# A two-layer decoder on one core: attention scores in four 64x64 tiles, normalisation after the value product, stage loops written out

## The chip, the cores and the metric

The kernel runs on one core of a Trainium2 chip. The metric is device time in microseconds for one execution. The kernel before takes 2339.52 us (median of three runs, 2339.38 to 2343.82). Engines are named as in the profile: PE is TensorE, PEld its weight loads, DVE VectorE, ACT ScalarE, POOL GpSimd, SP SyncE, and ACTq the queue from which ScalarE issues transfers.

## The reference

Sixty-four sequences of 64 tokens with 128 channels go through six sublayers, each with a residual: self-attention (16 heads of 8 channels, rotary, causal), a gated linear attention, a mixture of 15 routed experts and a shared one, self-attention with distance biases, a cross-attention, and a soft mixture of experts. The change is in the two self-attentions:

```python
scores = jnp.einsum('bhqd,bhkd->bhqk', q, k) / jnp.sqrt(jnp.float32(HEAD_DIM))
scores = scores + causal
attn = jax.nn.softmax(scores, axis=-1)
out = jnp.einsum('bhqk,bhkd->bhqd', attn, v)
out = out.transpose(0, 2, 1, 3).reshape(B, S, D_MODEL)
return out @ wo + bo
```

Layer 0 has biases on q, k, v and the output; layer 1 has none, but a term that falls with distance inside `scores`.

## The kernel before, in words

The 4096 tokens are 32 tiles of 128 rows, two sequences (b = 0, 1) in each. The stages follow one another: load and normalise (`load_and_norm`, lines 104 to 226), `attention` of layer 0, `mlstm`, `experts`, `attention` of layer 1, `cross_attention`, `soft_experts`. Each is a block in which every engine has its own program, written by hand as `turn(t, u)`, and engines meet only by semaphores. A turn works on several tiles at once, one step of each: it is a software pipeline whose order is the order of the code.

The first five of these stages are walked by one of two helpers. `unrolled` writes every turn out. `turns` writes out the first `head * ring` turns and the last `tail * ring`, and puts those between into a hardware loop (`Fori`) whose body is `ring` turns; there, tile numbers and semaphore counts come from registers. `load_and_norm` (ring 8), both attentions (ring 4, head 2, tail 2: turns 8 to 23 are looped), `mlstm` (ring 4, turns 8 to 27) and `experts` (8 groups of four tiles, ring 2, groups 2 to 5) use `turns`. `cross_attention` uses `unrolled`.

In turn t of `attention` the steps that matter here are:

- PE: transposes of the probabilities of tile t-1 (line 378, into `p_t[0]` and `p_t[1]`); output projection of tile t-2 (389); q and k of tile t+4 (400); v of tile t+2 (409); probabilities times values of tile t-1 (424, into `p_o`); a transpose for the normalised result (295); scores of tile t+2 (440 and 442). The scores have one buffer only: banks `p_s[0]` (heads 0 to 7) and `p_s[1]` (heads 8 to 15). Line 440 adds mask and bias and may not start before ACT has read the tile before out of the bank (semaphore `exped`). Line 442 multiplies q (64 rows of a sequence, 128 channels) by `kblk`, which holds k once for each of the 16 heads with all other heads' channels at zero, so that a contraction over 128 channels gives one head's score.
- DVE: row maxima of tile t+1 (459, 461) and the centring of the second half (465); residual of tile t-2 (472 adds the output bias in layer 0, 474 adds the projection); statistics; row sums of the second half of tile t (482); rotary terms of tile t+4 in layer 0 (491); 1/sum (498, 16 numbers a row); normalisation (285); probabilities of tile t times 1/sum (505, 1024 columns).
- ACT: copies of `p_t[0]` and `p_t[1]` of tile t-1 to `pT` (553, two of 512 columns); eight exponentials of tile t+1 with running sums (562); one exponential over the second half (566); in layer 1 the copies of q and k (573, 574); v to its blocks (582); `p_o` to `oT` of tile t-1 (590 or 592); input copy (598); `xnT` (301, 303).
- POOL: `kblk` of tile t+3, two instructions of 1024 columns (531), and 1/sqrt for the normalisation (271, 274).

Of the kernel before, what the change touches and what calls it, by code (L numbers as in the profile page):

```python
# [22 lines left out]
P = 128  # L23
B, S, D = 64, 64, 128
# [9 lines left out]


def turns(eng, turn, first, last, ring, n=NT, head=1, tail=1):

    for t in range(first, head * ring):
        turn(t, t % ring)
    with eng.Fori(head, n // ring - tail) as i:  # L40
        for u in range(ring):
            turn(i * ring + u, u)
    for t in range(n - tail * ring, last):
        turn(t, t % ring)
# [69 lines left out]
def load_and_norm(nc, g, io):  # L114
# [3 lines left out]
    with Mem(nc, "ld") as m:  # L118
# [20 lines left out]
        def _(dve):  # L139
# [26 lines left out]
            turns(dve, turn, -1, NT, R)  # L166

        @block.gpsimd
        def _(pool):
# [10 lines left out]
            turns(pool, turn, 0, NT, R)  # L180

        @block.tensor
        def _(pe):
# [12 lines left out]
            turns(pe, turn, 0, NT, R)  # L196

        @block.scalar
        def _(act):
# [26 lines left out]
            turns(act, turn, 0, NT, R)  # L226
# [86 lines left out]
def attention(nc, g, io, layer):  # L313
# [3 lines left out]
    with Mem(nc, f"at{layer}") as m:  # L317
        w = {n: m.sb(n, [P, P]) for n in names}
        heads = m.sb("heads", [P, NH])
# [5 lines left out]
        if rope:  # L325
# [22 lines left out]
        summed, inverted, probs_ready = m.sem("summed"), m.sem("inverted"), m.sem("probs_ready")  # L348
        pt_done, pt_copied, pv_done, oT_copied, y_done = (m.sem(n) for n in ("pt_done", "pt_copied", "pv_done", "oT_copied", "y_done"))
# [14 lines left out]
        def _(pe):  # L364
            pe.wait_ge(consts_in, 16 * len(loads))
            pe.wait_ge(zeroed, 1)
            wv = w["wv"][:, :].rearrange("i (j h d) -> i h j d", j=NH // 2, h=2)

            def turn(t, u):
                k, v = t - 1, (u - 1) % R  # L370
                if has(k):

                    pe.wait_ge(probs_ready, k + 1)
                    for hf in range(2):
                        if has(k - 1):
                            pe.wait_ge(pt_copied, 2 * k + hf - 1)
# [3 lines left out]
                        mm.then_inc(pt_done, 1)  # L380
                k = t - 2
                if has(k):

                    pe.wait_ge(oT_copied, k + 1)
# [18 lines left out]
                if has(k):  # L403

                    if has(k - 1):
                        pe.wait_ge(v_copied, 2 * k)
                    for h in range(2):
# [5 lines left out]
                if has(k):  # L413

                    pe.wait_ge(v_copied, 2 * (k + 1))
                    if has(k - 1):
                        pe.wait_ge(oT_copied, k)
                    pe.wait_ge(pt_copied, 2 * k + 2)
                    for c in range(4):
                        for b in range(PER):  # L420
# [12 lines left out]
                if has(k):  # L433
# [3 lines left out]
                    for hf in range(2):  # L437
# [8 lines left out]
            turns(pe, turn, first, last, R, head=2, tail=2)  # L446

        @block.vector
        def _(dve):
            dve.memset(vblk[:, :, :, :, :], 0.0).then_inc(zeroed, 1)  # L450
            dve.wait_ge(consts_in, 16 * len(loads))

            def turn(t, u):
                k, v = t + 1, (u + 1) % R
                if has(k):

                    scores = [p_s[hf][:, :].rearrange("p (h k) -> p h k", h=HH) for hf in range(2)]
# [1585 lines left out]
```

## Time and profile before

| | before |
|---|---|
| median of three runs | 2339.52 us |
| profiled execution, device time | 2340.49 us |
| its span | 2338.5 us |
| PE busy | 2044.0 us (87%) |
| DVE busy | 1645.1 us (70%) |
| ACT busy | 1514.4 us (65%) |
| POOL busy | 1249.6 us (53%) |

The span is the time from the first to the last instruction of the profile; device time has 2.0 us more around it. The busy time of PE is modelled: each matmul's end is an estimate, so ends overlap the next start, and the difference between two starts is what one step costs. An idle time in square brackets is shown before the instruction that ended it, with the instruction that it waited for.

### The profile page before, as it was taken

The numbers are of one execution on the slowest core, as the hardware profiler recorded it, in microseconds if no ns is written. First come the engines' busy times: TensorE is split into PE (matmuls) and PEld (weight loads), VectorE is DVE, ScalarE is ACT, GpSimd is POOL, SyncE is SP. The second block draws the span as 40 slices with busy tenths as digits, with TensorE's granted clock in tenths as the row PEclk, the third lists the DMA queues.
The fourth block names the chain that finished last, engine by engine and source line by source line (L and its number), as shares of the span: only waits on it lengthen the run. The fifth ranks groups of instructions, "written<-read, shape, count | busy, mean of one in ns | idle before, by whom it ended". The sixth has DMA issues, their size and how long they took to land. (4 is left out here: it accounts for less than half of the span.)

```text
span 2338.5 us, 64508 instructions
## 1 busy us (share of the span) xinstructions
PE 2044.0 (87%) x23034; PEld 1539.3 (66%) x23034; DVE 1645.1 (70%) x4478; ACT 1514.4 (65%) x4433; POOL 1249.6 (53%) x1444
## 2 busy tenths in 40 slices
PE   4899976646999999978996999996699999999899
PEld 2566563324666666745554888885588888888777
DVE  7799829976666666547775666665777777777567
ACT  4577726637777778857774777774776666666642
POOL 5777504445777778867773233320854544445430
PEclk9999956558999999989998999998899999999999
DMA  3000020011000000000000000001000000000101
GB/s 87 4 1 0 1 41 1 0 37 50 1 1 1 0 0 1 1 11 2 0 1 29 2 2 2 2 2 61 5 5 14 16 5 14 16 3 14 50 3 39
DMA packets 48919, 30.71 MB, mean 13 GB/s; under 512 B 21886, under 2 KB 46350, under 8 KB 48398
## 3 DMA queue, kind: packets, MB, share of 16 engines
q1 hardware_dynamic: 39438, 22.98, 3.5%
q10 hardware_dynamic: 9216, 4.20, 0.7%
q8 instruction: 166, 2.72, 0.5%
q14 instruction: 99, 0.81, 0.1%
HBM read 22.97 MB, written 4.19 MB: 12 GB/s over the span
## 5 line engine op out<-in xcount | busy, mean ns | idle before, releaser
L1006 POOL TENSOR_TENSOR ff_hl<-ff_hid,ff_hh 128x512 fp32r<-128x512 f32 x272 | 353.4, 1307 | 114.3 <-ACT ff_hh L1245 108.1
L1855 POOL TENSOR_TENSOR sm_zsum<-sm_zsum,sm_logits 128x512 f32<-128x512 f32 x120 | 154.7, 1289 | 275.3 <-ACT sm_logits L1881 273.6
L531 POOL TENSOR_TENSOR at_kblk<-at_kT,at_heads 128x1024 f32<-128x1024 f32 x128 | 242.0, 1912 | 101.5 <-PE at_p_s L442 91.8
L1174 DVE TENSOR_TENSOR ff_hid<-ff_p_b,ff_hid 128x512 f32<-128x512 f32 x240 | 164.3, 685 | 157.5 <-ACT ff_hid L1234 156.9
L1234 ACT ACTIVATE ff_hid<-ff_p_h,ff_b 128x512 f32<-128x512 f32 x272 | 185.6, 682 | 48.5 <-PE ff_p_h L1062 45.4
L1898 ACT ACTIVATE sm_sT<-sm_p_s 128x512 f32<-128x512 f32 x128 | 69.5, 595 | 221.1 <-PE sm_p_s L1691 221.1
L1245 ACT ACTIVATE ff_hh<-ff_hid 128x512 fp32r<-128x512 f32 x272 | 170.2, 626 | 40.8 <-DVE ff_hid L1174 38.7
L1867 POOL TENSOR_TENSOR sm_logits<-sm_logits,sm_peak 128x512 f32<-128x512 f32 x128 | 162.9, 1294 | 12.4 <-ACT sm_comb L1916 11.7
L1705 PE MATMUL sm_p_l<-g_phi,g_xnT 128*128 128x256 f32 x512 | 142.3, 405 | 26.8 <-ACT sm_logits L1926 25.6
L562 ACT ACTIVATE at_pr<-at_p_s,at_small 128x64 f32<-128x64 f32 x512 | 152.7, 341 | 4.6 <-DVE at_small L459 4.6
L1060 PE MATMUL ff_p_h<-ff_xh,ff_w1h 128*128 128x512 f32 x272 | 134.9, 496 | 12.1 <-ACT ff_hid L1234 8.5
L553 ACT ACTIVATE at_pT<-at_p_t 128x512 f32<-128x512 f32 x128 | 69.6, 595 | 112.8 <-PE at_p_t L378 112.8
L442 PE MATMUL at_p_s<-at_kblk,at_qT 128*64 128x512 f32 x512 | 139.5, 623 | 0.0
L1739 PE MATMUL sm_p_y<-sm_w,sm_sT 128*32 128x128 f32 x4096 | 125.4, 274 | 9.1 <-ACT sm_combT L1888 8.4
L1804 DVE TENSOR_REDUCE sm_rmax<-sm_p_l 128x2 f32<-128x512 f32 x128 | 88.3, 690 | 62.4 <-PE sm_p_l L1705 61.7
L1747 PE MATMUL sm_p_o<-sm_yy,sm_combT 128*64 128x129 f32 x2048 | 127.9, 276 | 2.5 <-issue 1.9
L1705 PEld LDWEIGHTS sm_p_l<-g_phi,g_xnT 128*128 128x128 f32 x512 | 91.1, 197 | 55.2 <-ACT sm_logits L1926 28.4
L1739 PE MATMUL sm_p_s<-sm_w,sm_sT 128*32 128x128 f32 x4096 | 124.1, 273 | 0.2 <-issue 0.2
L1739 PEld LDWEIGHTS sm_p_y<-sm_w,sm_sT 128*32 128x32 f32 x4096 | 107.6, 110 | 22.7 <-ACT sm_sT L1898 11.6
L1836 DVE TENSOR_TENSOR sm_yy<-sm_p_y,sm_wb 128x512 f32<-128x512 f32 x128 | 88.1, 692 | 49.1 <-PE sm_p_y L1739 49.0
L1747 PEld LDWEIGHTS sm_p_o<-sm_yy,sm_combT 128*64 128x64 f32 x2048 | 110.4, 136 | 17.1 <-DVE sm_yy L1836 13.3
L562 ACT ACTIVATION_READ_ACCUMULATOR at_pr<-at_p_s,at_small 128x1 f32 x512 | 120.6, 235 | 0.0
(302 smaller groups left out, 6079.8 us busy)
## 6 DMA issues: line engine op xcount, KB each, us to landing
sm_w<-in_w_soft SPq DMA_DIRECT2D x8, 512.0 KB, 3.6
ff_whole<-in_L_ffn_rW SPq DMA_DIRECT2D x30, 128.0 KB, 2.7
early_xs<-in_x ACTq DMA_DIRECT2D x32, 64.0 KB, 1.9
ld_ctx<-in_ctx ACTq DMA_DIRECT2D x32, 64.0 KB, 2.1
ml_vals<-in_ctx SPq DMA_DIRECT2D x8, 256.0 KB, 4.9
x_kept<-early_xs SPq DMA_DIRECT2D x1, 2048.0 KB, 7.4
g_xnT<-x_kept SPq DMA_DIRECT2D x1, 2048.0 KB, 9.4
out_x<-sm_acc SPq DMA_DIRECT2D x8, 256.0 KB, 2.3
```

Of the source, the lines that this page charges most:

```text
L442: mm = pe.matmul(p_s[hf][S * b:S * b + S, :], qT[:, v, b * S:(b + 1) * S], kblk[:, v % 2, b, hf * half:(hf + 1) * half], start=False, stop ...
L531: op = pool.tensor_tensor(kblk[:, v % 2, b, :].rearrange("p (h k) -> p h k", h=NH), row_bc(kT[:, v, b * S:(b + 1) * S], NH), col_bc(heads[ ...
L562: op = act.activation(pr[:, v, h * S:(h + 1) * S], p_s[0][:, h * S:(h + 1) * S], ACT.Exp, bias=small[:, v, 0, h:h + 1], accum_out=small[:, ...
L1006: eng.tensor_tensor(hl[:, q, :], hid[:, q, :], hh[:, q, :].bitcast(F32), ALU.subtract).then_inc(h_split, 1)
L1174: dve.tensor_tensor(h, p_b[e % 2][:, :], h, ALU.mult).then_inc(scaled, 1)
L1234: act.activation(hid[:, slot(u, c), :], p_h[c % 2][:, :], ACT.Gelu, bias=b1[:, c:c + 1]).then_inc(gelud, 1)
L1245: act.activation(hh[:, q, :], hid[:, q, :], ACT.Copy).then_inc(h_rounded, 1)
L1705: mm = pe.matmul(p_l[h][:, a * CW:(a + 1) * CW], xnT[:, t * P:(t + 1) * P], phi[:, c % 2, :], start=True, stop=True)
L1739: mm = pe.matmul((p_y, p_s)[j % 2][a][SP * k:SP * (k + 1), (b * CQ + q) * D:(b * CQ + q + 1) * D], sT[:, j % 2, a, b, n_ * SP:(n_ + 1) * S ...
L1747: mm = pe.matmul(p_o[j % 2][b * S:(b + 1) * S, a * E1:a * E1 + D + 1], combT[:, j % RING_C, q, a, b * S:(b + 1) * S], yy[:, j % 2, a * PER ...
L1855: pool.tensor_tensor(z, z, logits[:, j % RING_L, :, :], ALU.add).then_inc(summed, 1)
L1867: pool.tensor_tensor(here, here, row_bc(peak[:, c % 2, :], TU), ALU.subtract).then_inc(centred, 1)
```

## The change

It has three parts.

1. Scores. `kblk` is half as wide: heads 0 to 7 lie on partitions 0 to 63, heads 8 to 15 on partitions 64 to 127, 512 columns per sequence instead of 1024. PE adds mask and bias to both banks, then issues four matmuls of 64 rows by 64 columns of the array: row half hf writes bank `p_s[hf]`, column half b writes the rows of sequence b. `s_done` counts once per tile instead of twice. The constant `c_heads` has 8 columns.
2. Normalisation. The multiplication of the probabilities (line 505 of before) is gone. The reciprocal is written eight times for each head (`inv`, 128 columns instead of 16), PE transposes it by a matmul with the identity into `p_o[:, P:2P]`, ACT copies that to `invT`, and DVE multiplies the value product by it (`oT`), in place of ACT's copy of `p_o`. ACT takes the second `pT` copy between the fourth and the fifth exponential. In layer 0 the value bias goes into the output bias once, ahead of the loop, and POOL adds that bias to the residual.
3. Loops. `turns` is deleted; all five stages that used it are written out with `unrolled`. Semaphore counts and addresses become constants.

```diff
-            turns(dve, turn, -1, NT, R)
+            unrolled(dve, turn, -1, NT, R)
...
+        inv, invT = m.sb("inv", [P, 2, NH, HD]), m.sb("invT", [P, P])
...
-                    pe.wait_ge(probs_ready, k + 1)
                     for hf in range(2):
+                        pe.wait_ge(c_exped if hf else exped, k + 1)
...
+                    pe.wait_ge(inverted, k + 1)
+                    if has(k - 1):
+                        pe.wait_ge(oT_made, k)
+                    pe.matmul(p_o[:, P:2 * P], inv[:, v % 2, :, :].rearrange("p h d -> p (h d)"), g["ident"][:, :],
+                              start=True, stop=True).then_inc(inv_turned, 1)
...
-                        for b in range(PER):
-                            mm = pe.matmul(p_s[hf][S * b:S * b + S, :], qT[:, v, b * S:(b + 1) * S],
-                                           kblk[:, v % 2, b, hf * half:(hf + 1) * half], start=False, stop=True)
-                        mm.then_inc(s_done, 1)
+                    for b in range(PER):
+                        for hf in range(2):
+                            rows = slice(S * hf, S * hf + S)
+                            mm = pe.matmul(p_s[hf][S * b:S * b + S, :], qT[rows, v, b * S:(b + 1) * S],
+                                           kblk[rows, v % 2, b, :, :].rearrange("p h k -> p (h k)"), start=False, stop=True)
+                    mm.then_inc(s_done, 1)
...
-                    dve.reciprocal(small[:, v, 2, :], small[:, v, 1, :]).then_inc(inverted, 1)
+                    if has(k - 2):
+                        dve.wait_ge(inv_turned, k - 1)
+                    dve.reciprocal(inv[:, v % 2, :, :], col_bc(small[:, v, 1, :], HD)).then_inc(inverted, 1)
+                k = t - 1
+                if has(k):
+                    dve.wait_ge(pv_done, k + 1)
...
+                    dve.tensor_tensor(oT[:, (u - 1) % 2, :], p_o[:, 0:P], invT[:, :], ALU.mult).then_inc(oT_made, 1)
...
-                    dve.tensor_tensor(pr[:, v, :].rearrange("p (h k) -> p h k", h=NH), pr[:, v, :].rearrange("p (h k) -> p h k", h=NH),
-                                      col_bc(small[:, v, 2, :], S), ALU.mult).then_inc(probs_ready, 1)
...
+                turn_copy(t - 1, (u - 1) % 2, 0)
+                if has(t - 1):
+                    act.wait_ge(inv_turned, t)
...
+                    act.activation(invT[:, :], p_o[:, P:2 * P], ACT.Copy).then_inc(inv_copied, 1)
                 k, v = t + 1, (u + 1) % R
...
+                exps(k, v, range(HH // 2), False)
+                turn_copy(t - 1, (u - 1) % 2, 1)
+                exps(k, v, range(HH // 2, HH), True)
```

How this moves instructions in a steady turn of layer 0, engine by engine. On PE, from the scores of one tile to the projection, before (`at_` is the attention's prefix, `at0_` that of its semaphores in layer 0):

```order
L440 MATMUL at_p_s<-at_bias,at_pick 128x512 [waits at0_exped,at0_kblk_ready,at0_q_ready]
L442 MATMUL at_p_s<-at_kblk,at_qT 64x512 x2
L440 MATMUL at_p_s<-at_bias,at_pick 128x512 [waits at0_centred]
L442 MATMUL at_p_s<-at_kblk,at_qT 64x512 x2
L378 MATMUL at_p_t<-g_ident,at_pr 128x128 [waits at0_pt_copied,at0_probs_ready]
L378 MATMUL at_p_t<-g_ident,at_pr 128x128 x3
L378 MATMUL at_p_t<-g_ident,at_pr 128x128 [waits at0_pt_copied]
L378 MATMUL at_p_t<-g_ident,at_pr 128x128 x3
L389 MATMUL at_p_y<-at_wo,at_oT 128x128 [waits at0_n_copied,at0_x_made,at0_oT_copied]
```

and the same place of the changed kernel:

```order
L444 MATMUL at_p_s<-at_bias,at_pick 128x512 [waits at0_exped,at0_kblk_ready,at0_q_ready]
L444 MATMUL at_p_s<-at_bias,at_pick 128x512 [waits at0_centred]
L448 MATMUL at_p_s<-at_kblk,at_qT 64x512 x4
L374 MATMUL at_p_t<-g_ident,at_pr 128x128 [waits at0_pt_copied,at0_exped]
L374 MATMUL at_p_t<-g_ident,at_pr 128x128 x3
L374 MATMUL at_p_t<-g_ident,at_pr 128x128 [waits at0_pt_copied,at0_c_exped]
L374 MATMUL at_p_t<-g_ident,at_pr 128x128 x3
L381 MATMUL at_p_o<-g_ident,at_inv 128x128 [waits at0_oT_made,at0_inverted]
L391 MATMUL at_p_y<-at_wo,at_oT 128x128 [waits at0_n_copied,at0_x_made,at0_oT_made]
```

The four score matmuls stand together behind both bias matmuls, the transposes wait for ACT instead of DVE, and the transposition of 1/sum has come in ahead of the projection. On ACT, from the copies of `p_t` to the exponential of the second half, before:

```order
L553 ACTIVATE at_pT<-at_p_t 128x512 [waits at0_pv_done,at0_pt_done]
L550 REGISTER_ALU
L553 ACTIVATE at_pT<-at_p_t 128x512 [waits at0_pv_done,at0_pt_done]
L558 ISA
L562 ACTIVATE at_pr,at_small<-at_p_s,at_small 128x64 [waits at0_pt_done,at0_maxed]
L562 ACTIVATE at_pr,at_small<-at_p_s,at_small 128x64 x7
L566 ACTIVATE at_pr<-at_pr 128x512 [waits at0_centred]
```

and after:

```order
L569 ACTIVATE at_pT<-at_p_t 128x512 [waits at0_pv_done,at0_pt_done]
L588 ACTIVATE at_invT<-at_p_o 128x128 [waits at0_oT_made,at0_inv_turned]
L578 ACTIVATE at_pr,at_small<-at_p_s,at_small 128x64 [waits at0_pt_done,at0_maxed]
L578 ACTIVATE at_pr,at_small<-at_p_s,at_small 128x64 x3
L569 ACTIVATE at_pT<-at_p_t 128x512 [waits at0_pv_done,at0_pt_done]
L578 ACTIVATE at_pr,at_small<-at_p_s,at_small 128x64 [waits at0_pt_done,at0_maxed]
L578 ACTIVATE at_pr,at_small<-at_p_s,at_small 128x64 x3
L595 ACTIVATE at_pr<-at_pr 128x512 [waits at0_centred]
```

A copy of 128 columns that waits for PE's new matmul stands ahead of the exponentials, and the second `pT` copy stands between them. On DVE, the end of a turn, before:

```order
L498 RECIPROCAL at_small<-at_small 128x16 [waits at0_summed]
L285 TENSOR_SCALAR at_n_xn<-early_xs,at_n_mv,at_n_rstd 128x128 [waits at0_n_rstd_made0,at0_n_transposed]
L505 TENSOR_TENSOR at_pr<-at_pr,at_small 128x1024 [waits at0_inverted]
L459 TENSOR_REDUCE at_small<-at_p_s 128x8 [waits at0_s_done]
L461 TENSOR_REDUCE at_small<-at_p_s 128x8 [waits at0_s_done]
```

and after:

```order
L508 RECIPROCAL at_inv<-at_small 128x128 [waits at0_inv_turned,at0_summed]
L514 TENSOR_TENSOR at_oT<-at_p_o,at_invT 128x128 [waits at0_y_done,at0_pv_done]
L274 TENSOR_SCALAR at_n_xn<-early_xs,at_n_mv,at_n_rstd 128x128 [waits at0_n_rstd_made0,at0_n_transposed]
L469 TENSOR_REDUCE at_small<-at_p_s 128x8 [waits at0_s_done]
L470 TENSOR_REDUCE at_small<-at_p_s 128x8
```

The pass over 1024 columns is gone, the reciprocal has eight times the columns, and DVE has a new wait for PE's value product.

## Rows read from the trace of the kernel before

**Rows 1.** Windows: length, PE, PEld, DVE, ACT, POOL busy, clock, DMA.

```profile
130.00:241.30 111.30, 109.33 (x1105) 68.79 (x1104) 106.26 (x273) 81.52 (x385) 85.62 (x97) 1.00 0.00 1
380.00:480.00 100.00, 69.08 (x327) 33.94 (x327) 94.45 (x595) 60.75 (x232) 50.37 (x96) 0.55 0.00 0
```

**Rows 2.** Timeline, PE, one turn of layer 0: start, length, matmul records.

```profile
150.76 0.38 PE L440 MATMUL at_p_s<-at_bias,at_pick 128*128 128x512 bf16 x1
151.07 1.08 PE L442 MATMUL at_p_s<-at_kblk,at_qT 128*64 128x512 f32 x4
152.08 0.39 PE L440 MATMUL at_p_s<-at_bias,at_pick 128*128 128x512 bf16 x1
...
153.41 1.09 PE L378 MATMUL at_p_t<-g_ident,at_pr 128*128 128x128 f32 x8
154.34 0.39 PE L389 MATMUL at_p_y<-at_wo,at_oT 128*128 128x128 f32 x2
...
157.69 0.38 PE L440 MATMUL at_p_s<-at_bias,at_pick 128*128 128x512 bf16 x1
```

**Rows 3.** Timeline, ACT, the same turn; the last from layer 1.

```profile
154.10 1.09 ACT L553 ACTIVATE at_pT<-at_p_t 128x512 f32<-128x512 f32 x2 [1.79 <-PE at_p_t L378]
155.07 0.32 ACT L562 ACTIVATE at_pr<-at_p_s,at_small 128x64 f32<-128x64 f32 x1
...
1154.34 0.28 ACT L592 ACTIVATE at_oT<-at_p_o 128x128 f32<-128x128 f32 x1
```

**Rows 4.** Timeline, PE, first and last tile's first bias matmul, each layer.

```profile
70.62 0.61 PE L440 MATMUL at_p_s<-at_bias,at_pick 128*128 128x512 bf16 x1
...
282.69 0.38 PE L440 MATMUL at_p_s<-at_bias,at_pick 128*128 128x512 bf16 x1 [0.74 <-ACT at_pr L562]
...
1028.67 0.59 PE L440 MATMUL at_p_s<-at_bias,at_pick 128*128 128x512 bf16 x1
...
1245.71 0.38 PE L440 MATMUL at_p_s<-at_bias,at_pick 128*128 128x512 bf16 x1 [0.73 <-ACT at_pr L562]
```

**Rows 5.** Timeline, PE, in the cross-attention.

```profile
1405.32 0.40 PE L1386 MATMUL xa_pj<-xa_wvh,xa_zh 128*128 128x512 f32 x1
1405.56 0.39 PE L1387 MATMUL xa_pj<-xa_wvl,xa_zh 128*128 128x512 f32 x1
...
1406.54 1.10 PE L1333 MATMUL xa_p_s<-xa_kT,xa_qT 64*64 64x128 f32 x32
1407.58 0.33 PE L1344 MATMUL xa_p_t<-g_ident,xa_pr 128*128 128x128 f32 x1
```

**Rows 6.** Groups by shape: count, busy, mean ns, idle before, what ended it.

```profile
L1788 DVE RECIPROCAL sm_rz<-sm_p_l 128x256 f32<-128x256 f32 x8 | 14.1, 1757 | 5.6 <-PE sm_p_l L1676 5.6
```

**Rows 7.** Timeline, DVE, layer 0.

```profile
151.72 1.49 DVE L505 TENSOR_TENSOR at_pr<-at_pr,at_small 128x1024 f32<-128x1024 f32 x1
```

**Rows 8.** Waits, PE for DVE, while layer 0's attention drains (283:304).

```profile
PE at_p_t L378 <- DVE at_pr L505: 3.5, 2, 1.8
```

**Rows 9.** Timeline, PE, load stage: two written-out turns, then one looped.

```profile
16.29 0.45 PE L192 MATMUL ld_tp<-g_ident,ld_xn 128*128 128x128 f32 x1
...
18.32 0.45 PE L192 MATMUL ld_tp<-g_ident,ld_xn 128*128 128x128 f32 x1
...
25.14 0.48 PE L192 MATMUL ld_tp<-g_ident,ld_xn 128*128 128x128 f32 x1 [0.60 <-ACT early_cnT L223]
...
26.64 0.48 PE L192 MATMUL ld_tp<-g_ident,ld_xn 128*128 128x128 f32 x1 [0.60 <-ACT early_cnT L223]
```

**Rows 10.** Waits, DVE, looped part of `mlstm`: us in total, times, longest.

```profile
DVE ml_dd L758 <- issue: 1.7, 4, 0.4
```

**Rows 11.** Timeline, PE, experts: first hidden matmul of groups 2, 6, 7.

```profile
659.32 0.49 PE L1060 MATMUL ff_p_h<-ff_xh,ff_w1h 128*128 128x512 f32 x1 [0.18 <-ACT ff_hid L1234]
...
892.91 0.50 PE L1060 MATMUL ff_p_h<-ff_xh,ff_w1h 128*128 128x512 f32 x1
...
950.88 0.50 PE L1060 MATMUL ff_p_h<-ff_xh,ff_w1h 128*128 128x512 f32 x1
```

More of the change, by code:

```diff
@@ L33, in has @@
     return not isinstance(k, int) or 0 <= k < n
[L36 to L44, printed above, removed]
 def unrolled(eng, turn, first, last, ring):
@@ L178, in turn @@
                 pool.tensor_tensor(rstd[:, u, :], rstd[:, u, :], g["neghalf"][:, 0:2], ALU.pow).then_inc(rstd_made, 1)
-            turns(pool, turn, 0, NT, R)
+            unrolled(pool, turn, 0, NT, R)
         @block.tensor
@@ L194, in turn @@
                 pe.transpose(bank[:, 2 * P:3 * P], cn[:, u, :], g["ident"][:, :]).then_inc(transposed, 1)
-            turns(pe, turn, 0, NT, R)
+            unrolled(pe, turn, 0, NT, R)
         @block.scalar
@@ L224, in turn @@
                                scale=g["gbx"][:, 0:1]).then_inc(copied, 1)
-            turns(act, turn, 0, NT, R)
+            unrolled(act, turn, 0, NT, R)
 class Norm:
@@ L366, in _ @@
             pe.wait_ge(zeroed, 1)
+            if rope:
+                pe.wait_ge(bv_spread, 1)
+                pe.matmul(p_v[:, 0:D], bvb[:, :], w["wo"][:, :], start=True, stop=True).then_inc(bv_done, 1)
             wv = w["wv"][:, :].rearrange("i (j h d) -> i h j d", j=NH // 2, h=2)
@@ L502, in turn @@
                     norm.dve_norm(dve, t - 3, (u - 1) % 2, 1)
-                if has(k):
-                    dve.wait_ge(inverted, k + 1)
-                    dve.tensor_tensor(pr[:, v, :].rearrange("p (h k) -> p h k", h=NH), pr[:, v, :].rearrange("p (h k) -> p h k", h=NH),
-                                      col_bc(small[:, v, 2, :], S), ALU.mult).then_inc(probs_ready, 1)
-            turns(dve, turn, first, last, R, head=2, tail=2)
+            unrolled(dve, turn, first, last, R)
         @block.gpsimd
@@ L537, in turn @@
                     norm.pool_rstd(pool, t - 3, (u - 1) % 2, 1)
-            turns(pool, turn, first, last, R, head=2, tail=2)
+            unrolled(pool, turn, first, last, R)
         @block.scalar
@@ L600, in turn @@
                     norm.act_copy(act, t - 2 - levels, p_y[:, P:2 * P])
-            turns(act, turn, first, last, R, head=2, tail=2)
+            unrolled(act, turn, first, last, R)
 MH, MD = 4, 32
@@ L719, in turn @@
                     mm.then_inc(pv_done, 1)
-            turns(pe, turn, first, last, R, head=2)
+            unrolled(pe, turn, first, last, R)
         @block.vector
@@ L827, in turn @@
                     norm.dve_stats(dve, n, w)
-            turns(dve, turn, first, last, R, head=2)
+            unrolled(dve, turn, first, last, R)
         @block.gpsimd
@@ L853, in turn @@
                     norm.pool_rstd(pool, t - 3, (u - 1) % 2)
-            turns(pool, turn, first, last, R, head=2)
+            unrolled(pool, turn, first, last, R)
         @block.scalar
@@ L905, in turn @@
                     norm.act_copy(act, t - 5, p_n[:, 0:P])
-            turns(act, turn, first, last, R, head=2)
+            unrolled(act, turn, first, last, R)
 NE, TOPK = 15, 3
@@ L1103, in turn @@
                         pe.transpose(p_n[:, 0:P], norm.xn[:, q % 2, 0, :], g["ident"][:, :]).then_inc(norm.transposed, 1)
-            turns(pe, turn, first, last, R, NGR)
+            unrolled(pe, turn, first, last, R)
         FIRST_SPLIT = {-1: [NC_FF - 1], 0: [1, 2, 3, 4]}
@@ L1186, in turn @@
                         router[c - 5]()
-            turns(dve, turn, first, last, R, NGR)
+            unrolled(dve, turn, first, last, R)
         @block.gpsimd
@@ L1197, in turn @@
                     split_hidden(pool, t, u, c)
-            turns(pool, turn, first, last, R, NGR)
+            unrolled(pool, turn, first, last, R)
         @block.scalar
@@ L1259, in turn @@
                         norm.act_copy(act, 4 * (t - 1) + AT_LNT.index(c), p_n[:, 0:P])
-            turns(act, turn, first, last, R, NGR)
+            unrolled(act, turn, first, last, R)
 XH, XD = 8, 64
```

85 lines of the change are left out of this document (47 added, 38 removed).

## The prediction, made before the changed kernel ran

> **What bounds the kernel now.** I read the windows by stage first, then one turn of an attention on each engine, then the prices of what is new. In the looped part of layer 0's attention PE is busy 109 of 111 us and DVE 106 of 111 [rows 1], so either could pass for the limit. The timeline shows a third thing, a circle through one buffer. Follow one turn. PE starts the first bias matmul at 150.76 and the transposes 2.65 us later, at 153.41 [rows 2]; four of them release ACT's first copy at 154.10, 0.69 later; the two copies take 0.97 up to the first exponential at 155.07 [rows 3]; and the last exponential frees the bank for PE's next bias matmul at 157.69, 2.62 later [rows 2, 3]. The sum, 2.65 + 0.69 + 0.97 + 2.62 = 6.93, is the whole turn. Nothing in it is idle, and PE's other work (projection, q, k, v, value product) lies beside it. Where there is less of that work the wait is in the open: PE idles 0.74 and 0.73 us for ACT's exponentials before the last tile's scores of each layer [rows 4]. From first to last tile, 31 intervals, layer 0 takes 212.07 us and layer 1 217.04 [rows 4]. The 4.97 us more in layer 1 I put down to transposes that wait for DVE's 1024-column pass, as they openly do at the end of layer 0 (3.5 us in two waits [rows 8]).
>
> **The score part.** Now a bias matmul, two tiles of 64 columns side by side, and both once more: 2.65 us. After: bias, bias, four tiles. Two 512-column matmuls of one mode that follow each other start 0.24 apart (1405.32, 1405.56 [rows 5]); from a bias matmul to tiles it is 0.31, and two tiles take 1.01 (151.07 to 152.08) [rows 2]. Whether four take the same is the open price. Two matmuls of 512 columns in 1.01 us are 0.126 us per matmul of 128 columns, two at a time. The cross-attention issues 16 matmuls of 64x64 with 128 columns (32 records, two a matmul), to two banks in the same pattern: at two at a time they would take 2.02 us, and they take 1.04 (1406.54 to 1407.58 [rows 5]). So four run side by side, and I take 1.01; the other bound is 2.02. Scores: 0.24 + 0.31 + 1.01 = 1.56, that is 1.09 less.
>
> The Trainium skill (TensorEngine Tiling, Key Properties) says that changing the tiling mode drains the array; the trace agrees in that 0.31 stands where the mode changes and 0.24 where it doesn't. Without that rule the second bias matmul would be 0.31 and the turn 0.07 longer, some 4 us in all.
>
> **What comes into the circle.** PE's transposition of 1/sum stands where the projection stood, 0.93 us behind the start of the transposes (153.41 to 154.34), and is 0.39 long like it [rows 2]. The release of ACT costs 0.06: eight transposes in 1.09 end 0.28 behind their last start, so the fourth ends at 0.63, and ACT starts at 0.69 [rows 2, 3]. The copy of 1/sum can thus start at 1.56 + 0.93 + 0.39 + 0.06 = 2.94. The first `pT` copy starts at 1.56 + 0.69 = 2.25 and takes half of 0.97, up to 2.73; ACT idles 0.21. The new copy of 128 columns is 0.28 long [rows 3]; copies start 0.11 sooner than they are long (0.60 against 0.485 [rows 3]), so 0.17: 3.11. The exponentials take 2.62 and the second `pT` copy between them 0.49: 6.22. That is the turn I forecast, 0.71 less than 6.93. The value product needs the second copy, which now is done 0.6 us later than the first half of the product would like it; its first half covers that.
>
> **Do the others fit into 6.22?** PE: 6.93 less 1.09, plus some 0.25 for the new matmul, is 6.1. DVE is busy 106.26 / 16 = 6.64 a turn [rows 1]. It loses 1.49 (the 1024-column pass [rows 7]) and the bias add, at least an eighth of that, 0.19. It gains a multiplication of 128 columns, some 0.3, and seven eighths of a reciprocal of 128 columns. A reciprocal is dear: 1757 ns for 256 columns [rows 6], half is 0.88, so 0.8 more. Sum 6.1, close below. POOL is busy 85.62 / 16 = 5.35 [rows 1] and halves its largest instruction. ACT, 81.52 / 16 = 5.1 [rows 1], swaps one copy for another.
>
> **Attentions, summed.** The first three intervals of a layer are a ramp without all parts of the circle; I leave them as they are. Layer 0: 28 x 0.71 = 19.9 us. Layer 1: the same and the 4.97 us, since transposes no longer wait for DVE: 24.9. At the drain of each layer 3.5 us of waits for the pass [rows 8] go, and a reciprocal longer by 0.7 takes their place: 2.8 each, 5.6. The folded bias costs a DVE copy and a matmul ahead of layer 0's first q, which nothing hides: 0.6 against me. Together 49.8.
>
> **Loops written out.** In the load stage ACT issues two transfers a turn between its copies. Written-out turns there take (18.32 - 16.29) / 2 = 1.015 us; looped ones, with the same work and with addresses from registers, 1.50 (25.14 to 26.64), and PE waits for ACT [rows 9]. All 16 looped turns become written-out ones: 7.8 us. This is no detail of the attentions and the surest term. In `mlstm` DVE is the limit (94 of 100 us [rows 1]) and loses 1.7 us at four loop ends [rows 10]. In the experts four looped groups take (892.91 - 659.32) / 4 = 58.40 and a written-out one 950.88 - 892.91 = 57.97 [rows 11]: 1.7. Together 11.2. That written-out code costs anything itself I see nowhere: the load stage and the experts run both kinds, and the written-out one is never slower [rows 9, 11].
>
> **The sum.** 49.8 + 11.2 = 61.0 us. The profiled execution took 2340.5 us (span 2338.5 and 2.0 around it), so 2279.5; it lay 1.0 above the median of the three runs, so the forecast is 2278.5.
>
> **Rivals.**
>
> 1. *Another engine closes in.* DVE's 6.1 is within 0.1 of the circle, built on lengths of one trace; its new wait for the value product stands ahead of the normalisation. At 6.4 to 6.8 a turn the gain shrinks by 60 x 0.2 to 0.6: 2290 to 2313. For it: the narrow margin. Against: the pass that leaves DVE was its longest. Chance 0.20.
> 2. *Less than 6.22.* If ACT doesn't idle the 0.21 and layer 1, with two q and k matmuls fewer, runs more freely, 6.0: another 13 us, 2265. Chance 0.15.
> 3. *Tiles of 512 columns share something that tiles of 128 don't.* Then 2.02 instead of 1.01: a turn is 7.23, 0.30 above now; layer 0 loses 8.4, layer 1 (7.11 now) 3.4, and with drains, loops and the folded bias 2340.5 + 11.8 - 5.6 - 11.2 + 0.6 = 2336, less 1.0: 2335. Nothing in the trace speaks for it but that it isn't shown. Chance 0.03.
> 4. *Reading the banks decides, not writing them.* If the circle went only through ACT, quicker scores would bring nothing and 0.38 would be added: 7.31 a turn, 28 x 0.38 + 28 x 0.20 = 16.2 lost there, 2339.5. PE's first bias matmul starts right behind the last exponential in every turn, which speaks against it. The Trainium skill (TensorEngine Tiling, PSUM Bottleneck) warns of this: tiles speed up the array but not the emptying of its banks. Chance 0.02.
> 5. *The clock, on the slow side.* With PE 69 of 100 us busy in `mlstm` its granted clock is 0.55, about the lower level of 1.2 GHz; in the attention it is 1.00 [rows 1]. If four tiles for one count as less work and the clock falls, PE's 6.1 a turn become about 11, +4 a turn against now, from a fifth of the 60 turns on slower than before; in half of them 2340 + 120 - 17 = about 2440. Against: the cross-attention has such tiles, and PE stays some 95% busy. Chance 0.03.
>
> The forecast keeps 0.57.
>
> **How the numbers follow.** A measurement of this kernel tells from no change what is over 0.2%, 4.7 us. Faster: forecast, 1 and 2 with 0.92 and half of 3, 0.94 in all; within 0.2%: the rest of 3 and 4, 0.03; slower 0.03. Range: a turn of 6.0 in both layers gives 2265, of 6.5 gives 2295; drains and folded bias add some 3 either way. With part of rival 1 I give 2262 to 2304.
>
> **What would show each step.** The first bias matmuls of neighbouring tiles 6.2 us apart in both layers; 32-tile spans of about 192 us; four score tiles in 1.0 us; a reciprocal of 0.8 to 1.0 us; ACT's `invT` copy behind a wait of 0.2 for PE; turns of 1.0 us throughout the load stage, which then ends near 44 instead of 52 us; no issue gap on DVE in `mlstm`. The prediction is wrong if score tiles take 2 us, if PE's first bias matmul is released by something else than the last exponential, if DVE has no idle time in a turn, or if the clock in an attention falls.

## The result, and the profile after

The changed kernel takes 2278.3 us (median of four runs, 2276.1 to 2279.0), against 2339.5 us before. The ratio is 0.9731, with a 95% interval of 0.9718 to 0.9743: 61 us faster by the medians, 63 by the ratio (60 to 66). The forecast was 2278.5. The total fits better than its terms: two errors of about 5 us nearly cancel, and that is luck. Stages end where ACT starts its last copy into `g_xnT` (the last one with the span):

| stage | before | after | difference | forecast |
|---|---|---|---|---|
| load | 51.4 | 48.0 | -3.3 | -7.8 |
| attention 0 | 253.8 | 227.5 | -26.2 | -22.1 |
| mlstm | 209.7 | 209.4 | -0.3 | -1.7 |
| experts | 501.6 | 500.0 | -1.6 | -1.7 |
| attention 1 | 255.1 | 226.5 | -28.5 | -27.7 |
| cross-attention | 334.4 | 334.3 | -0.1 | 0 |
| soft experts | 732.6 | 730.8 | -1.8 | 0 |

The last two stages were not touched. In the ten other kernels below the last one lies between 728.3 and 732.8 us, so its 1.8 here says nothing, and one profile doesn't settle differences of a few us in so long a stage.

**The circle.** PE's rows of one turn of layer 0, to be laid beside [rows 2] (start, length, matmul records), with the row of the weight loads ahead:

```profile
147.83 0.13 PEld L444 LDWEIGHTS at_p_s<-at_bias,at_pick 128*128 128x128 bf16 x2 [0.29 <-issue]
...
148.08 0.38 PE L444 MATMUL at_p_s<-at_bias,at_pick 128*128 128x512 bf16 x1 [0.35 <-POOL at_qT L532]
148.38 1.09 PE L448 MATMUL at_p_s<-at_kblk,at_qT 64*64 64x512 f32 x8
149.40 1.09 PE L374 MATMUL at_p_t<-g_ident,at_pr 128*128 128x128 f32 x8
150.33 0.39 PE L381 MATMUL at_p_o<-g_ident,at_inv 128*128 128x128 f32 x2
...
154.25 0.38 PE L444 MATMUL at_p_s<-at_bias,at_pick 128*128 128x512 bf16 x1 [0.34 <-POOL at_qT L532]
```

There are two weight loads of L444 but one matmul: the record of the first bias matmul is missing, and the row at 148.08 is the second. I therefore date the first by its weight load, 147.83. (In the kernel before, where both records are there, the weight load at 150.73 starts 0.03 ahead of its matmul.) Four tiles take 1.02 us (148.38 to 149.40; forecast 1.01), the scores 1.54 to 1.57 in all (forecast 1.56), and from turn to turn it is 6.17 (148.08 to 154.25; forecast 6.22). ACT in the same turn, beside [rows 3]:

```profile
147.46 0.26 ACT L578 ACTIVATION_READ_ACCUMULATOR at_pr<-at_p_s,at_small 128x1 f32 x1
...
150.09 0.60 ACT L569 ACTIVATE at_pT<-at_p_t 128x512 f32<-128x512 f32 x1 [0.80 <-PE at_p_t L374]
150.75 0.28 ACT L588 ACTIVATE at_invT<-at_p_o 128x128 f32<-128x128 f32 x1
150.93 0.31 ACT L578 ACTIVATE at_pr<-at_p_s,at_small 128x64 f32<-128x64 f32 x1
...
152.09 0.62 ACT L569 ACTIVATE at_pT<-at_p_t 128x512 f32<-128x512 f32 x1
```

The first copy starts 0.69 behind the transposes, the copy of 1/sum 0.66 later (its idle time, 0.18, is what is left of 0.66 when the first copy's 0.485 is taken off), the exponentials 0.18 after that. The last exponential ends at 147.72, and PE's next weight load starts at 147.83. The profile puts PE's idle time down to POOL's `qT`, which is a misreading: POOL is two tiles ahead of PE there, so the q for these scores was made two turns earlier, and in layer 1 the same gap is put down to ACT's exponentials (below, 1191.08). First and last tile of each layer, beside [rows 4]:

```profile
67.85 0.63 PE L444 MATMUL at_p_s<-at_bias,at_pick 128*128 128x512 bf16 x1 [0.33 <-issue]
...
259.20 0.38 PE L444 MATMUL at_p_s<-at_bias,at_pick 128*128 128x512 bf16 x1 [0.35 <-ACT at_pr L578]
...
997.60 0.63 PE L444 MATMUL at_p_s<-at_bias,at_pick 128*128 128x512 bf16 x1 [0.33 <-issue]
...
1191.08 0.38 PE L444 MATMUL at_p_s<-at_bias,at_pick 128*128 128x512 bf16 x1 [0.35 <-ACT at_pr L578]
```

31 intervals take 191.4 and 193.5 us, 20.7 and 23.6 less than before; the layers now differ by 2 us only, from their first three turns.

**The other engines.** Windows of after, layer 0 and layer 1 (columns as in [rows 1]), and DVE's rows that answer to the prediction's prices:

```profile
120.00:250.00 130.00, 122.73 (x1479) 91.89 (x1498) 115.93 (x337) 109.99 (x507) 86.56 (x148) 1.00 0.01 2
1030.00:1180.00 150.00, 137.21 (x1593) 97.34 (x1618) 126.61 (x412) 138.92 (x630) 83.91 (x145) 1.00 0.01 2
```

```profile
147.81 0.94 DVE L508 RECIPROCAL at_inv<-at_small 128x128 f32<-128x128 f32 x1
148.67 0.23 DVE L514 TENSOR_TENSOR at_oT<-at_p_o,at_invT 128x128 f32<-128x128 f32 x1
...
149.54 0.69 DVE L469 TENSOR_REDUCE at_small<-at_p_s 128x8 f32<-128x512 f32 x1 [0.39 <-PE at_p_s L448]
```

The reciprocal takes 0.94 us (0.86 from row to row, forecast 0.88). DVE has 0.39 idle in each turn of layer 0 (8.1 us in 21 turns) and about 0.48 in layer 1, waiting for the scores, and the clock stays at 1.00.

### The profile page after: what moved, and what is told of

Same layout as the page of the kernel before. It is cut to its first block and busy times, and to the rows that moved or that the text cites. A ratio compares the mean times of both kernels' runs of the same rounds, so it can differ in the third digit from the quotient of the medians.

```text
span 2276.6 us, 62556 instructions
## 1 busy us (share of the span) xinstructions
PE 1997.3 (88%) x23071; PEld 1551.1 (68%) x23164; DVE 1593.3 (70%) x4448; ACT 1525.7 (67%) x4433; POOL 1152.6 (51%) x1476
## 5 line engine op out<-in xcount | busy, mean ns | idle before, releaser
L543 POOL TENSOR_TENSOR at_kblk<-at_kT,at_heads 128x512 f32<-128x512 f32 x128 | 130.7, 1042 | 106.5 <-PE at_p_s L448 96.9
L1759 PEld LDWEIGHTS sm_p_s<-sm_w,sm_sT 128*32 128x32 f32 x4096 | 113.4, 110 | 2.3 <-issue 2.3
L428 PE MATMUL at_p_o<-at_pT,at_vblk 128*32 128x64 f32 x2048 | 104.5, 222 | 9.8 <-ACT at_pT L569 8.6
```

The lines of the kernel that those rows point to most:

```text
L543: op = pool.tensor_tensor(kblk[:, v % 2, b, :, :], row_bc(kT[:, v, b * S:(b + 1) * S], HH), col_bc(heads[:, :], S), ALU.mult)
L1759: mm = pe.matmul((p_y, p_s)[j % 2][a][SP * k:SP * (k + 1), (b * CQ + q) * D:(b * CQ + q + 1) * D], sT[:, j % 2, a, b, n_ * SP:(n_ + 1) * S ...
```

## The experiments

Each ratio is to the kernel before on the same chip; "us" behind a ratio is its difference from 1 (or from another ratio) times 2339.5. A difference of two ratios carries both intervals, 4 to 5 us either way for most pairs here; where it is smaller than that, only the stages and turns in the profiles speak. Turns are read from PE's rows.

**Loops alone** (e1), the kernel before with `unrolled` in all stages:

```diff
-            turns(dve, turn, first, last, R, head=2, tail=2)
+            unrolled(dve, turn, first, last, R)
```

> The kernel before with every loop written out, nothing else. From the trace of after, the stages that only lost their loops gave 3.4 us (load), 0.3 (mlstm) and 1.7 (experts); the attentions' turns that end a loop are 0.08 longer than the others, some 1 us in all. So 6 us less than before, about 2333.5 (2331 to 2335). The prediction's terms would make it 11.2 less, 2328. If it is 2339, writing out brings nothing and the stages differ for another reason.

Ratio 0.9969 (0.9957 to 0.9981): 7.3 us, 4.4 to 10.1. The forecast's 11.2 lies outside. By itself the interval doesn't say whether it is 5 or 10; the load stage ends at 48.3, as in the changed kernel, and `mlstm` takes 209.3 us, as there (209.4).

**Scores alone** (e2), on top of e1: four tiles, the 1024-column pass kept.

```diff
-                        for b in range(PER):
-                            mm = pe.matmul(p_s[hf][S * b:S * b + S, :], qT[:, v, b * S:(b + 1) * S],
-                                           kblk[:, v % 2, b, hf * half:(hf + 1) * half], start=False, stop=True)
+                    for b in range(PER):
+                        for hf in range(2):
+                            rows = slice(S * hf, S * hf + S)
+                            mm = pe.matmul(p_s[hf][S * b:S * b + S, :], qT[rows, v, b * S:(b + 1) * S],
+                                           kblk[rows, v % 2, b, :, :].rearrange("p h k -> p (h k)"), start=False, stop=True)
```

> The kernel before with loops written out and the score tiles of after; the probabilities are still scaled by the 1024-column pass. My theory: two limits lie close together, the circle (6.93 less 1.09 = 5.84) and DVE's own work with the pass in it. DVE then sets the turn: about 6.65 in layer 0 and 6.45 in layer 1 (5.55 busy and 0.9 of waits for POOL), in all 28 us less than with loops written out alone: 2305 (2298 to 2318). If the parts of the change simply add up, the scores bring 56 x 1.09 = 61 us: 2272. If PE's score time were worth nothing, 2333.

Ratio 0.9807 (0.9789 to 0.9826): 38 us less than e1, more than the 28 that I expected and far from 61. Layer 0 takes 6.62 a turn (expected 6.65), with DVE never waiting: 123.71 of 130 us busy, the rest being the distances between its instructions. One row shows more than my sum had:

```profile
130.00:260.00 130.00, 108.69 (x1316) 78.28 (x1333) 123.71 (x333) 99.05 (x466) 97.06 (x119) 1.00 0.01 2
```

```profile
181.58 0.67 DVE L473 TENSOR_TENSOR early_xs<-early_xs,at_bo 128x128 f32<-128x128 f32 x1
182.28 0.29 DVE L475 TENSOR_TENSOR early_xs<-at_p_y,early_xs 128x128 f32<-128x128 f32 x1
```

Two additions of one size, 0.67 and 0.29 long; the long one has both operands in SBUF and lies beside POOL's `kblk` (180.06 to 182.10). Layer 1 takes 6.18, not 6.45: there DVE isn't the limit, but a circle of 5.84 in which the transposes wait a little for the pass:

```profile
1099.98 0.38 PE L440 MATMUL at_p_s<-at_bias,at_pick 128*128 128x512 bf16 x1 [0.78 <-ACT at_pr L563]
1100.29 1.09 PE L444 MATMUL at_p_s<-at_kblk,at_qT 64*64 64x512 f32 x8
1101.65 1.09 PE L378 MATMUL at_p_t<-g_ident,at_pr 128*128 128x128 f32 x8 [0.27 <-DVE at_pr L506]
...
1106.16 0.38 PE L440 MATMUL at_p_s<-at_bias,at_pick 128*128 128x512 bf16 x1 [0.78 <-ACT at_pr L563]
```

I had counted 0.9 a turn of DVE's waits for POOL as fixed; in this window of 140 us they sum to 7.0, 0.3 a turn.

**Normalisation alone** (e3), the changed kernel with the e2 piece undone.

> The changed kernel with the old score matmuls (128-row contraction, two column tiles a half). DVE has lost its 1024-column pass, PE has its old scores. My theory: the circle is 2.65 + 2.94 - 1.56 + 0.17 + 2.62 + 0.49, about 7.27 a turn, longer than in the kernel before (6.93 and 7.11): 14 us more, less 8.8 in the drains: 2339 (2334 to 2343), although DVE is freed of 1.5 us and nothing was added to PE but one 128-column matmul. If instead DVE's pass was the limit, the turn is at most 6.93 in both layers: 2325 or less.

Ratio 0.9990 (0.9980 to 1.0000): 2 us less than the kernel before, and 5 us more than e1. Each turn takes 7.28 in both layers (forecast 7.27). PE's rows show the old scores inside the new circle; again the first bias matmul has no record:

```profile
151.18 1.08 PE L446 MATMUL at_p_s<-at_kblk,at_qT 128*64 128x512 f32 x4 [0.44 <-ACT at_pr L577]
152.19 0.39 PE L444 MATMUL at_p_s<-at_bias,at_pick 128*128 128x512 bf16 x1
152.51 1.08 PE L446 MATMUL at_p_s<-at_kblk,at_qT 128*64 128x512 f32 x4
153.52 1.09 PE L374 MATMUL at_p_t<-g_ident,at_pr 128*128 128x128 f32 x8
```

DVE has lost its longest pass, and yet the turns are longer than those of e1 (6.93 in layer 0, mostly 6.93 to 7.27 in layer 1). Over e1 the scores alone bring 38 us, the normalisation alone costs 5, and both together bring 56: 23 us belong to neither. The scores alone shorten the circle by 1.09 but run into DVE's pass (e2); the normalisation takes that pass away but adds 0.35 to the circle, where nothing else has left it (e3).

**The copy of 1/sum sooner** (e4), the changed kernel with PE's transposition between the halves:

```diff
                         mm.then_inc(pt_done, 1)
-
-                    pe.wait_ge(inverted, k + 1)
-                    if has(k - 1):
-                        pe.wait_ge(oT_made, k)
-                    pe.matmul(p_o[:, P:2 * P], inv[:, v % 2, :, :].rearrange("p h d -> p (h d)"), g["ident"][:, :],
-                              start=True, stop=True).then_inc(inv_turned, 1)
+                        if hf == 0:
+                            pe.wait_ge(inverted, k + 1)
+                            if has(k - 1):
+                                pe.wait_ge(oT_made, k)
+                            pe.matmul(p_o[:, P:2 * P], inv[:, v % 2, :, :].rearrange("p h d -> p (h d)"), g["ident"][:, :],
+                                      start=True, stop=True).then_inc(inv_turned, 1)
```

> The changed kernel with PE's transposition of 1/sum put between the two halves of the transposes, so that ACT can copy it straight behind the first pT copy without its idle 0.18. Circle theory: the turn is 0.18 shorter, 5.99, and the kernel 10 us faster than the changed one: 2268 (2266 to 2272). Rival: PE, which shows only some 0.2 to 0.3 idle a turn, is the limit, or DVE with its 0.39 idle is: then the turn stays at 6.1 to 6.17 and the time at 2275 to 2278.

Ratio 0.9683 (0.9664 to 0.9701), 11 us less than the changed kernel; a turn is 5.99 in both layers. ACT's copies now lie back to back:

```profile
153.17 0.60 ACT L570 ACTIVATE at_pT<-at_p_t 128x512 f32<-128x512 f32 x1 [0.81 <-PE at_p_t L374]
153.66 0.27 ACT L589 ACTIVATE at_invT<-at_p_o 128x128 f32<-128x128 f32 x1
153.82 0.32 ACT L579 ACTIVATE at_pr<-at_p_s,at_small 128x64 f32<-128x64 f32 x1
```

The circle is still the limit: in layer 0 PE stands idle 0.26 in each turn ahead of the bias matmuls, and DVE waits 0.25 for the scores (5.4 us in 22 turns).

**POOL's multiplication moved** (e5), the changed kernel; in `mlstm`, POOL makes `rdiag` (by `spread`, the same instruction) behind the first of its two rstd steps and when DVE has begun its turn, and tile 0's ahead of all turns:

```diff
-                k = t + 3
-                if has(k):
-                    if has(k - 2):
-                        pool.wait_ge(x_done, k - 1)
-                    pool.tensor_tensor(rdiag[:, (u + 3) % 2], row_bc(diag[:, :], MH),
-                                       col_bc(uu[:, bass.ds(k, 1), :].rearrange("p a h -> p (a h)"), S), ALU.mult).then_inc(r_ready, 1)
...
+                k = t + 4
+                if has(k):
+                    if has(k - 2):
+                        pool.wait_ge(x_done, k - 1)
+                    if has(t + 2):
+                        pool.wait_ge(d_step, D_STEPS * (t + 2) + 1)
+                    spread(k, u % 2)
```

> The changed kernel with one POOL instruction of mlstm moved: the 128x256 multiplication that makes rdiag now waits until DVE has begun its turn and runs beside DVE's operations that read PSUM or one operand, not beside DVE's subtraction at L796. Theory: with the loops written out the two came to lie on each other, and DVE's subtraction takes 0.59 instead of 0.41 in 25 turns, which gave back most of the 1.7 us of loop ends. Then L796 takes 0.41 again, the turn is 4.98 instead of 5.15, and mlstm is 4.3 us shorter: 2274 against 2278.3. Rival: L796 is long for another reason (what it waits for, or the new code as such), stays at 0.59, and the time stays.

Ratio 0.9706 (0.9693 to 0.9719), 6 us less than the changed kernel, and `mlstm` is 5.0 shorter in the profile. The changed kernel, POOL and then DVE:

```profile
347.33 0.61 POOL L861 TENSOR_TENSOR ml_rdiag<-ml_diag,ml_uu 128x256 f32<-128x256 f32 x1
...
346.31 0.42 DVE L778 TENSOR_TENSOR ml_dd<-ml_p_x,ml_causal 128x256 f32<-128x256 f32 x1
347.64 0.59 DVE L796 TENSOR_TENSOR ml_dd<-ml_dd,ml_sm 128x256 f32<-128x256 f32 x1
351.46 0.42 DVE L778 TENSOR_TENSOR ml_dd<-ml_p_x,ml_causal 128x256 f32<-128x256 f32 x1
```

The kernel of e5, where it begins its turn at 350.12 and the next at 355.10 (4.98 instead of 5.15):

```profile
350.69 0.61 POOL L857 TENSOR_TENSOR ml_rdiag<-ml_diag,ml_uu 128x256 f32<-128x256 f32 x1 [0.66 <-DVE ml_dd L778]
...
350.12 0.42 DVE L778 TENSOR_TENSOR ml_dd<-ml_p_x,ml_causal 128x256 f32<-128x256 f32 x1
351.44 0.42 DVE L796 TENSOR_TENSOR ml_dd<-ml_dd,ml_sm 128x256 f32<-128x256 f32 x1
355.10 0.42 DVE L778 TENSOR_TENSOR ml_dd<-ml_p_x,ml_causal 128x256 f32<-128x256 f32 x1
```

**Transfers from SP** (e6), the changed kernel; the load stage's `dma_start` calls moved from ACT to SP with the same waits on `transposed` and `normed`.

> The changed kernel with the load stage's 64 transfers issued by SP instead of ACT. Theory: DVE with its own work and POOL's reply (1.17 and 1.30 alternating) sets the turn once the loops are written out, not ACT as the prediction had it: ACT loses all its issuing and the stage stays at 48.0 us within 0.7, the time at 2278. Rival: ACT with its transfers is still the limit (the prediction's view): a turn falls from 1.2 to 0.9 and the stage is 6 us or more shorter.

Ratio 0.9731 (0.9714 to 0.9748), the same as the changed kernel. The stage ends at 46.7 instead of 48.0, but only because it starts 1.3 us sooner (PE's first transpose at 7.48 instead of 8.77). After the first turns the intervals are 1.17 and 1.30 in turn, as in the changed kernel. Those of the changed kernel:

```profile
37.26 0.45 PE L181 MATMUL ld_tp<-g_ident,ld_xn 128*128 128x128 f32 x1 [0.43 <-DVE ld_cn L152]
...
38.42 0.45 PE L181 MATMUL ld_tp<-g_ident,ld_xn 128*128 128x128 f32 x1 [0.29 <-issue]
...
39.73 0.44 PE L181 MATMUL ld_tp<-g_ident,ld_xn 128*128 128x128 f32 x1 [0.43 <-DVE ld_cn L152]
```

**A second reciprocal** (e8), the changed kernel; DVE also writes an unused `spare`:

```diff
+                    dve.reciprocal(spare[:, v % 2, :, :], col_bc(small[:, v, 1, :], HD))
                     dve.reciprocal(inv[:, v % 2, :, :], col_bc(small[:, v, 1, :], HD)).then_inc(inverted, 1)
```

> The changed kernel with a second, unused reciprocal of 128 columns on DVE in each turn of the attentions (0.87 from start to start). It asks how near the rival was that DVE closes in. DVE idles 0.39 a turn in layer 0 and 0.46 in layer 1, waiting for the scores. Theory: the circle sets the turn and DVE's slack is just that idle time, so the turn grows by 0.48 in layer 0 and 0.41 in layer 1, to 6.65 and 6.58, and the kernel by some 25 us: 2303. If DVE had no slack (DVE is the real limit), a turn grows by the whole 0.87: 2327. If it had more than it shows, 2278 to 2290.

Ratio 0.9874 (0.9859 to 0.9890), 33 us more than the changed kernel, not 25. Layer 0 has turns of 6.66 (expected 6.65). Layer 1 is uneven: of its last 28 intervals ten are 6.17, five 6.66 to 6.70, and thirteen lie between 7.33 and 8.40, seven of these at 7.66; no side of my expectation had that. In a turn of 7.66 POOL and DVE show:

```profile
1071.01 2.04 POOL L545 TENSOR_TENSOR at_kblk<-at_kT,at_heads 128x512 f32<-128x512 f32 x2 [0.94 <-PE at_p_s L449]
...
1071.28 0.86 DVE L274 TENSOR_SCALAR at_n_xn<-early_xs,at_n_mv,at_n_rstd 128x128 f32<-128x128 f32 x1
1072.06 1.08 DVE L274 TENSOR_SCALAR at_n_xn<-at_n_xn,at_n_mv,at_n_rstd 128x128 f32<-128x128 f32 x1
```

The second L274 of a tile takes 1.07 to 1.12 us in 14 of the layer's 32 tiles and 0.34 or 0.35 in the others.

**The same with `kblk` later** (e9), on top of e8:

```diff
                         pool.wait_ge(s_done, k - 1)
+                    if has(t + 1):
+                        pool.wait_ge(maxed, 2 * (t + 1) + 1)
```

> The kernel with two reciprocals, and POOL's kblk multiplications (2.04 us a turn) held back until DVE has done its first maximum, so that they run beside DVE operations that read PSUM. In the kernel with two reciprocals layer 0 took 6.66 a turn, as expected, but layer 1 mostly 7.66: there DVE's two normalisations (L274) lie beside kblk and take 0.86 and 1.08 instead of 0.34 each. Theory: DVE is held up by POOL's instruction, 1.0 us and more a turn; with kblk moved both take 0.34 again, layer 1's turns are at most 6.7, and the kernel is some 9 us faster than with two reciprocals alone: 2304 (2301 to 2306). Rival: DVE is late for another reason and the turns of 7.66 stay, 2313 or more.

Ratio 0.9792 (0.9776 to 0.9808): 19 us less than with two reciprocals alone, twice what I expected. Layer 1 falls to 6.39 a turn, and layer 0 to 6.51 (there L274 had been 0.48 beside `kblk`). The same two instructions:

```profile
1103.48 0.33 DVE L274 TENSOR_SCALAR at_n_xn<-early_xs,at_n_mv,at_n_rstd 128x128 f32<-128x128 f32 x1
1103.73 0.34 DVE L274 TENSOR_SCALAR at_n_xn<-at_n_xn,at_n_mv,at_n_rstd 128x128 f32<-128x128 f32 x1
```

**Loops kept** (e10), the changed kernel with `turns` put back in all its places.

> The changed kernel with the hardware loops of before put back in all stages, the attention's arithmetic as changed. The prediction's terms give the loops 11.2 us: 2289.5. What the stages of the two traces show is 3.4 (load), 0.3 (mlstm) and 1.7 (experts), with a little in the attentions 6: 2284 (2281 to 2287). Rival: the written-out code costs as much elsewhere (instruction fetch) and the difference is nothing, 2278.

Ratio 0.9751 (0.9733 to 0.9768), 4.7 us more than the changed kernel, which the two intervals together don't tell from nothing; but the load stage ends at 51.6, 3.6 later. The forecast's 11.2 would be 0.9779, outside.

**Together** (e7): the edits of e4, e5 and e6.

> The changed kernel with three edits together: the transposition of 1/sum between the halves (0.18 a turn in 56 turns, 10 us), POOL's multiplication in mlstm moved (4.3 us), and the loads on SP (0). If they add up: 14.5 us less than the changed kernel, 2264. If one of them meets a new limit, 2267 to 2274.

Ratio 0.9675 (0.9661 to 0.9688), 13 us less than the changed kernel and the fastest here; 14.5 were expected, which the interval holds. That it beats e4 (0.9683) is not shown by these runs; its `mlstm` is shorter by 4.8 in the profile.

## Why the prediction came out right, step by step

- **The circle as the limit: right.** It was tried from four sides: 7.28 with the old scores (e3, 7.27 expected), 6.17 with the new (6.22), 5.99 with ACT's idle 0.18 taken out (e4, 5.99), and 6.66 where DVE is made longer than the circle (e8, layer 0, 6.65).
- **Four tiles side by side: right,** 1.02 us against 1.01. Reading 128-column tiles of another stage [rows 5] was enough. Rival 3 falls with it; rival 4 falls with the turn of 6.17 instead of 7.31, and rival 5 with the clock of 1.00.
- **ACT's idle time for the copy of 1/sum:** 0.18, forecast 0.21. The 0.05 a turn that is missing in 6.22 lies in such small distances. e4 shows rival 2's condition made true: without that idle time the turn is 5.99, and rival 2 had said 6.0.
- **Layer 1 "the same and the 4.97 us, since transposes no longer wait for DVE": right in kind.** Both layers have 6.17; before, layer 1 had between 6.93 and 7.36. Of 24.9 us 23.6 came.
- **Rival 1, DVE closing in:** its slack is the 0.39 us that it idles, and in layer 0 e8 shows the bill as this and no more. I had it at 0.1, too near: the bias add, which I took at 0.19, is 0.50 to 0.66 long in 25 of 32 tiles of the kernel before (L472).
- **The drains were mis-sized.** I took 3.5 us of waits [rows 8] less a reciprocal longer by 0.7, 2.8 a layer. What went is 5.9 in layer 0 and 5.2 in layer 1, from the last tile's first bias matmul to the stage's end. Transposes of before's and after's drain:

```profile
285.34 1.09 PE L378 MATMUL at_p_t<-g_ident,at_pr 128*128 128x128 f32 x8
290.72 1.09 PE L378 MATMUL at_p_t<-g_ident,at_pr 128*128 128x128 f32 x8 [1.83 <-DVE at_pr L505]
295.95 1.09 PE L378 MATMUL at_p_t<-g_ident,at_pr 128*128 128x128 f32 x8 [1.68 <-DVE at_pr L505]
...
304.61 0.48 PE L295 MATMUL at_p_y<-g_ident,at_n_xn 128*128 128x128 f32 x1 [1.59 <-DVE at_n_xn L285]
```

```profile
260.52 1.09 PE L374 MATMUL at_p_t<-g_ident,at_pr 128*128 128x128 f32 x8
...
264.86 1.04 PE L374 MATMUL at_p_t<-g_ident,at_pr 128*128 128x128 f32 x8
...
268.00 1.04 PE L374 MATMUL at_p_t<-g_ident,at_pr 128*128 128x128 f32 x8
...
275.03 0.47 PE L284 MATMUL at_p_y<-g_ident,at_n_xn 128*128 128x128 f32 x1 [1.73 <-DVE at_n_xn L274]
```

  The last tile's scores are 1.1 shorter; two drain turns take 7.5 instead of 10.6, since the transposes wait for the exponentials alone and sum, reciprocal and pass have left the chain; and from the last transposes to the end it is 7.0 instead of 8.7. The reciprocal, which I charged with 0.7 a turn, holds PE up only once, by 0.24 in the last of these turns. I also left the last tile's shorter scores out.
- **The load stage was the term that failed:** "All 16 looped turns become written-out ones: 7.8 us", "the surest term". It gave 3.3. The written-out turns of 1.015 from which I took the price are those of an engine catching up. PE's third tile had come 3.46 us behind its second, since ACT first issued transfers and loaded a table (its first copy starts at 12.56), and DVE had worked on in that time. DVE's own rows beside these turns are 1.24 apart:

```profile
15.61 0.32 DVE L161 TENSOR_SCALAR ld_xn<-early_xs,ld_mv,ld_rstd 128x128 f32<-128x128 f32 x1
16.85 0.35 DVE L161 TENSOR_SCALAR ld_xn<-early_xs,ld_mv,ld_rstd 128x128 f32<-128x128 f32 x1
```

  Written out, DVE with its own operations and POOL's answer keeps these 1.24 a tile through the whole stage (PE's 1.17 and 1.30 in turn), and that is the floor. The last turns of before ran faster still (two in 1.85), again with work that DVE had already done. e6 shows that ACT's issuing is no longer in the way. I had read which engine was waited for, and not how fast the next one behind it was.
- **`mlstm` gave 0.3 of 1.7, since the gain went into a new collision.** The four loop ends are gone, but DVE's L796 is 0.58 or 0.59 long in 22 of the 32 tiles, where before it was 0.41 or 0.42 in half of them and 0.47 to 0.51 in ten. Writing out alone does this: e1 has the same 22, and e10, with its loops, doesn't. e5 shows the cause: move POOL's instruction, and it is 0.42. (Its gain of 5.0 is more than was lost, since the kernel before had part of this collision too.) Three turns are longer by 0.2 to 0.35 as well, at the same turns in e5; DVE stands still there with no wait that the profile names. Every kernel with this stage written out has such turns, at other places in e1, e2, e8 and e9; in the looped turns of e10 the long ones lie at the loop ends. In these runs, then, they go with the written-out code; what makes DVE stand still there isn't shown.
- **The experts:** six intervals between groups are 0.9 shorter, not 1.7, since one of them is 58.8 where the others are 58.0. It is so in e3 to e7, and not in e1, e2, e8 and e9, which have the stage written out too; this stays open. So does what lengthens single turns of the written-out attentions (6.35 and 6.37 in the changed kernel): e10, with its loops, has none above 6.19 among its steady turns, but neither has e4, which is written out. That "the written-out one is never slower" was too strong.
- **The folded bias** can't be told from the ramp: first scores 19.4 us into the stage instead of 19.3.

The errors are 4.5 and 1.4 us too much for load and `mlstm`, and 5.5 us too little for the drains. The mechanism of the attentions carried the forecast; that it came within 1 us is the cancelling of these errors.

## What to carry to other kernels

Look for the circle through a single buffer and add up its links, even where PE and DVE look 95% busy: where it was the limit it gave the turn to within 0.05 us (changed kernel, e3, e4). A part of a change can cost time alone (here 5 us) and bring time beside another part (here 18 us), so cost the turn with both and with each. For every engine that becomes faster, work out the next limit behind it before you multiply the gain by the number of turns, and look at what POOL and DVE will do at the same moment once their phases move.

## What the runs showed of the hardware

- A POOL instruction with operands in SBUF holds up some DVE instructions that lie beside it: a normalisation of 128 columns took 0.86 and 1.08 us beside a POOL multiplication of two times 1.02, and 0.33 and 0.34 away from it (e8, e9); a subtraction of 256 columns 0.59 against 0.42 (e5). DVE's reductions and operations that read PSUM lay beside the same instructions at their usual length (in the changed kernel L469 at 149.54 is 0.69 and L470 at 150.15 is 0.68 long, with `kblk` from 149.65 to 151.69). In e8 the two DVE instructions end at 1072.14 and 1073.14, about 0.1 behind the ends of POOL's two (1071.01 and 2.04 more is 1073.05). The Trainium skill (SBUF — State Buffer, Who interferes with whom) says that DVE and GpSimd share a pair of ports under a lock that is held for a whole instruction, and that it binds DVE where an instruction has two SBUF inputs or runs in a mode that uses both pairs; the trace agrees, by these ends and by the reductions that weren't held up; which mode the normalisation ran in it doesn't show.
- The hold-up works the other way too. In e2 POOL's sum for `kT` (L525, 128 columns) takes 1.70 us in 26 of 32 tiles, where the changed kernel has 0.45 or 0.46. In one such turn it runs from 184.90 to 186.60, and DVE's 1024-column pass from 185.07 to 186.29. The pass itself takes 1.22 us in e2, and in the kernel before 1.22 in 33 tiles and 1.49 in 23.
- A reciprocal of 128 columns takes 0.94 us, four times a multiplication of 128 columns with one factor in PSUM (0.23).
- In the changed kernel and in all ten others made here one of the two bias matmuls' records is missing for 61 of 64 tiles, also where the loops are kept (e10); the kernel before has them all. A first start then has to be read from the weight loads.
